# The self stage of an attention and expert kernel rewritten: unnormalised q, x in four parts, early splits of the context weights

## The chip, the cores and the metric

One core of a Trainium2 chip. The metric is device time in microseconds: the time of one execution of the whole program. The core has five engines that run their own instruction streams and meet at semaphores: PE (TensorE, matmuls and transposes), DVE (VectorE), ACT (ScalarE), POOL (GpSimd) and SP (SyncE, which here only issues transfers). PEld is TensorE's loading of weights.

## The reference, cut to what matters

Eight sequences of 256 tokens with 256 features, and for each a context of 1601 rows. The program computes four blocks: grouped-query attention over the tokens and the context, a two-of-eight expert layer, an attention over the context, and a one-of-eight expert layer. The change touches the first block, and a ring of the last. The first block is

```python
x = x + xattn(_layernorm(x), ctx_2048, wq, wk, wv, wo, wk_ctx, wv_ctx, q_norm_w, k_norm_w)

q = rms_norm((x @ wq).reshape(B, L, 16, 128), q_norm_w)     # rsqrt(mean(q*q) + eps) * q * w, for each head
k = rms_norm((x @ wk).reshape(B, L, 4, 128), k_norm_w)
v = (x @ wv).reshape(B, L, 4, 128)
k_ctx, v_ctx = rms_norm(h @ wk_ctx), h @ wv_ctx
q = q * cos + rotate_half(q) * sin
k = k * cos + rotate_half(k) * sin
scores = einsum('blhd,bmhd->bhlm', q, concat(k_ctx, k)) / sqrt(128) + mask
out = einsum('bhlm,bmhd->blhd', softmax(scores), concat(v_ctx, v)) @ wo
```

The rotation is linear in q, and the rms of q is one number for a token and a head. It can be applied to q, or to the scores of that token and head.

## The kernel before, in words

The 2048 tokens are 16 tiles of 128. The stages of the first block follow each other, each in a scope of its own; at a scope's end all engines meet, the stores are waited for, and semaphores are cleared.

**Self stage** (`self_projections`, from line 113). It makes q, k and v of the tokens. A matmul in fp32 quality is done as three with operands split into a high and a low part: ACT makes the high part by a copy (`high`, `split_w`), VectorE the low one by a subtraction (`low`, line 332). A tile has five granules (`GRAN`): j = 0 is k (and v beside it), j = 1 to 4 are four heads of q each, 512 columns a granule. For a granule, TensorE makes `ps_p` (`project`), ACT squares it head by head with a sum (line 239), POOL turns the sums into `rms` by a power of -0.5 (lines 372 and 376), VectorE multiplies `ps_p` by `rms` into `normed` (line 294), makes two halves `by_sin` (line 302) and one head of `by_cos` (line 308), POOL the other three heads of `by_cos` (line 383), VectorE adds them into `roped` (line 317), TensorE transposes it into `ps_t` (line 450), ACT copies that to `out_t` (line 249), and SP stores it in HBM. Each engine's order is written out by hand, with TensorE four granules ahead (`LEAD`), seven of eight tile pairs inside or beside a hardware loop. Before the first granule x (one transfer) gets its statistics, and SP has issued all weights and tables in a row.

**Constants.** A short block of its own casts three constant matrices for later stages (lines 2553 to 2561).

**Context stage** (`context_projections`, from line 472). It loads and splits its weights `w_raw`, `w_hi`, `w_lo`, and does for 104 tiles of context rows: project k and v (twelve matmuls), square (line 589), sum (650), root on POOL (703 and 707), normalise (657), four transposes (745), copy with the weight of k as a scale (597), copy of v (592), stores. Its last two bodies of four tiles split `wo` beside that.

**Attention** (`attention`, from line 806), written out for 32 pairs of sequence and k head. It begins by splitting the first q, k and v. A unit is two heads of one tile of 128 tokens, 128 units in all, eight slots each. For a head, TensorE makes scores in four pieces (lines 1138 to 1143), VectorE takes the maximum of each piece (983) and of the four with a minus sign (`neg_max`, 990), ACT makes four exponentials with `neg_max` as bias (899), POOL divides by the sum (1083), TensorE transposes (1156), ACT and VectorE split (911, 1009), and TensorE multiplies with v (1176 to 1178). The score piece p of a head waits for the exponential p of the head before it. In slots 3 and 7 of a unit the fourth piece of a head is made; in slot 7 it stands right behind the third on TensorE. In slot 6 of even units VectorE also adds the projected output to x (`add_y`, 1025).

**Last stage** (`moe_slots`, from line 2353): 23 slots of 128 rows. POOL gathers the rows of a slot into `xg` and scatters `made`; a gather of slot s + 4 is issued behind the scatter of slot s (`RING = LEAD = 4`), and VectorE's normalise of slot s + 2 (2485), which waits for the gather, stands ahead of the copy `ht` (2511) that TensorE's output product `ps_y` (2435) needs.

Of the kernel before, what the change touches and what calls it, by code (L numbers as in the profile page):

```python
# [10 lines left out]
ALU = mybir.AluOpType  # L11
# [98 lines left out]
LN_EPS, RMS_EPS = 1e-5, 1e-6  # L110


def self_projections(nc, x_sb, x_loaded, ident_loaded, half_made, w_dram, rope_dram, qw_dram, kw_dram, q_dram, k_dram, v_dram,
                     mean_var, rstd, half, ident):
    wq_d, wk_d, wv_d = w_dram
    with ExitStack() as ctx:
        sb, psum, sem = scope(ctx, nc)
        norm = norm_memory(sb, sem, "norm1")
        w_raw = sb("w1_raw", [P, DC, W1])
        w_hi = sb("w1_hi", [P, DC, W1], F32R)  # L120
        w_lo = sb("w1_lo", [P, DC, W1], F32R)
        rope = sb("rope", [P, 2, QT, HD])
# [6 lines left out]
        sq_sum = sb("sq_sum1", [P, GRAN, GRP])  # L129
        sq_mean = sb("sq_mean1", [P, GRAN, GRP])  # L130
        rms = sb("rms1", [P, GRAN, GRP])
        normed = sb("normed1", [P, GRAN, GRP * HD])
        by_cos = sb("by_cos", [P, GRAN, GRP * HD])
        by_sin = sb("by_sin", [P, GRAN, GRP * HD])
        roped = sb("roped", [P, GRAN, GRP * HD])
# [7 lines left out]
        tab_loaded = sem("tab_loaded")  # L143
        w_hi_done, w_lo_done = sem("w1_hi_done"), sem("w1_lo_done")
# [4 lines left out]
        square_done, mean_done, rms_done = sem("square1"), sem("mean1"), sem("rms1s")  # L149
        normed_done, cos_done, sin_done, roped_done = sem("normed1s"), sem("cos1"), sem("sin1"), sem("roped1")  # L150
        t_done, copied, sum_taken = sem("t1_done"), sem("t1_copied"), sem("sum1_taken")
        v_copied, store_begun = sem("v1_copied"), sem("store1_begun")
# [3 lines left out]
        NB = NT // 2  # L156
        LAST = NB - 1
        WPIECES = W1 // 512
        w_loaded = [sem(f"w1_loaded{j}") for j in range(WPIECES)]

        def granule(f):

            return (f // GRAN) % 2, f % GRAN
# [6 lines left out]
        LEAD = 4  # L170
        LASTG = 2 * GRAN
        CH = 3

        def exists(f, last):
            return not (last and f >= LASTG)

        with nc.Block() as block:
            @block.sync
            def _(sp):
                w_rows = [w.rearrange("(c p) n -> p c n", p=P) for w in (wk_d, wv_d, wq_d)]  # L180
                for j in range(WPIECES):
                    src = w_rows[j] if j < 2 else w_rows[2][:, :, (j - 2) * 512:(j - 1) * 512]
                    sp.dma_start(w_raw[:, :, j * 512:j * 512 + 512], src).then_inc(w_loaded[j], 16)
# [2438 lines left out]
```

## Time and profile before

| | us |
|---|---|
| Median of 3 runs | 3123.14 |
| Lowest and highest | 3123.08, 3124.46 |
| The profiled execution, its own time | 3123.67 |
| Its span in the profile | 3121.9 |
| PE busy | 2891.9 (93%) |
| DVE busy | 2181.1 (70%) |
| ACT busy | 2030.9 (65%) |
| POOL busy | 1612.4 (52%) |

Busy time is summed over an engine's instructions, where they overlap once. Matmuls are pipelined, so a busy PE says that it had work, and not how fast it went. The gap between the span and the execution's own time lies before the first and behind the last recorded instruction.

### The profile page before, as it was taken

How to read it: one execution, taken by the hardware profiler on the slowest of the kernel's cores; microseconds unless marked ns; L12 is line 12 of the kernel's file. 1: busy time of each engine (PE TensorE's matmuls, PEld its weight loads, DVE VectorE, ACT ScalarE, POOL GpSimd, SP SyncE). 2: the span in 40 equal slices, each digit the busy share in tenths (PEclk: the TensorE clock that was granted, in tenths of full speed). 3: DMA queues.
4: the chain of work that ended last, by engine and by line, in shares of the span. 5: the costliest groups of instructions: out<-in, count | busy, mean ns of one | idle time of the engine just before them, and what ended most of it. 6: DMA issues, size and time to landing. Idle time of an engine off the chain costs nothing. (4 is left out here: it accounts for less than half of the span.)

```text
span 3121.9 us, 61580 instructions
## 1 busy us (share of the span) xinstructions
PE 2891.9 (93%) x18731; PEld 2450.3 (78%) x18731; DVE 2181.1 (70%) x4611; ACT 2030.9 (65%) x5169; POOL 1612.4 (52%) x2087
## 2 busy tenths in 40 slices
PE   5887999899999999999999999999999977699698
PEld 4665888678888888888888888888888854388654
DVE  7995444577777777777777777777777767766443
ACT  5664666677777777777777777777777647666111
POOL 6993333455555555555555555555555344465122
PEclk9998999999999999999999999999999979899699
DMA  4335666610110110110110110110110010353511
GB/s 134 116 118 175 202 202 203 201 62 33 52 46 33 53 46 33 52 46 33 53 46 33 52 46 33 53 46 33 53 46 33 1 46 1 99 158 113 177 33 28
DMA packets 244462, 236.02 MB, mean 76 GB/s; under 512 B 11654, under 2 KB 224527, under 8 KB 244208
## 3 DMA queue, kind: packets, MB, share of 16 engines
q1 hardware_dynamic: 225552, 212.01, 20.7%
q10 hardware_dynamic: 16448, 15.73, 1.7%
q0 software_dynamic: 2208, 5.12, 0.6%
q8 instruction: 132, 2.16, 0.3%
q14 instruction: 122, 1.00, 0.1%
HBM read 148.93 MB, written 84.80 MB: 75 GB/s over the span
## 5 line engine op out<-in xcount | busy, mean ns | idle before, releaser
L911 ACT ACTIVATE pt_hi<-ps_t 128x512 fp32r<-128x512 f32 (+2 forms) x1024 | 570.4, 557 | 412.9 <-PE ps_t L1156 409.7
L983 DVE TENSOR_REDUCE piece_max<-ps_s 128x1 f32<-128x512 f32 (+2 forms) x1024 | 631.7, 622 | 257.1 <-PE ps_s L1143 229.5
L1009 DVE TENSOR_TENSOR pt_lo<-ps_t,pt_hi 128x512 fp32r<-128x512 f32 (+2 forms) x1024 | 656.4, 641 | 200.5 <-ACT pt_hi L911 184.3
L1083 POOL TENSOR_SCALAR prob<-prob,inv_sum 128x512 f32<-128x512 f32 (+2 forms) x1024 | 639.4, 645 | 268.5 <-DVE inv_sum L999 268.5
L899 ACT ACTIVATE prob<-ps_s,neg_max 128x512 f32<-128x512 f32 (+2 forms) x1024 | 649.2, 634 | 87.6 <-DVE neg_max L990 70.9
L1176 PE MATMUL ps_o<-pt_hi,v_hi 128*128 128x256 f32 (+1 forms) x1856 | 595.4, 321 | 0.0
L1156 PE MATMUL ps_t<-ident,prob 128*128 128x128 f32 (+1 forms) x3712 | 571.9, 272 | 1.4 <-DVE pt_lo L1009 1.3
L1178 PE MATMUL ps_o<-pt_hi,v_lo 128*128 128x256 f32 (+1 forms) x1856 | 523.2, 282 | 0.0
L1177 PE MATMUL ps_o<-pt_lo,v_hi 128*128 128x256 f32 (+1 forms) x1856 | 522.3, 281 | 0.0
L1156 PEld LDWEIGHTS ps_t<-ident,prob 128*128 128x128 f32 (+1 forms) x3712 | 456.2, 140 | 60.7 <-issue 1.6
L1138 PE MATMUL ps_s<-k_hi,q_hi 128*128 128x512 f32 (+2 forms) x1024 | 403.8, 394 | 35.0 <-ACT prob L899 20.0
L1143 PE MATMUL ps_s<-k_hi,q_lo 128*128 128x512 f32 (+2 forms) x1024 | 397.0, 388 | 0.0
L1139 PE MATMUL ps_s<-k_lo,q_hi 128*128 128x512 f32 (+2 forms) x1024 | 376.9, 368 | 0.0
L1177 PEld LDWEIGHTS ps_o<-pt_lo,v_hi 128*128 128x128 f32 (+1 forms) x1856 | 353.6, 191 | 0.0
L1176 PEld LDWEIGHTS ps_o<-pt_hi,v_hi 128*128 128x128 f32 (+1 forms) x1856 | 352.0, 190 | 0.0
L1178 PEld LDWEIGHTS ps_o<-pt_hi,v_lo 128*128 128x128 f32 (+1 forms) x1856 | 349.9, 189 | 0.0
L1091 POOL TENSOR_TENSOR k_lo<-raw_k,k_hi 128x480 fp32r<-128x480 f32 x124 | 150.0, 1219 | 251.3 <-ACT k_hi L918 251.3
L1098 POOL TENSOR_TENSOR v_lo<-raw_v,v_hi 128x512 fp32r<-128x512 f32 (+1 forms) x128 | 155.1, 1220 | 241.2 <-ACT v_hi L925 241.1
L1138 PEld LDWEIGHTS ps_s<-k_hi,q_hi 128*128 128x128 f32 x1024 | 194.3, 190 | 75.3 <-ACT prob L899 55.7
L1143 PEld LDWEIGHTS ps_s<-k_hi,q_lo 128*128 128x128 f32 x1024 | 197.0, 192 | 22.8
L899 ACT ACTIVATION_READ_ACCUMULATOR prob<-ps_s,neg_max 128x1 f32 x1024 | 208.8, 204 | 0.0
L1139 PEld LDWEIGHTS ps_s<-k_lo,q_hi 128*128 128x128 f32 x1024 | 195.1, 191 | 2.9
(262 smaller groups left out, 5621.4 us busy)
## 6 DMA issues: line engine op xcount, KB each, us to landing
v_scratch<-v_out SPq DMA_DIRECT2D x120, 256.0 KB, 2.5
raw_k<-k_scratch SPq DMA_DIRECT2D x32, 960.0 KB, 5.3
raw_v<-v_scratch SPq DMA_DIRECT2D x32, 960.0 KB, 4.7
k_scratch<-k_out SPq DMA_DIRECT2D x104, 256.0 KB, 2.6
q_scratch<-out_t SPq DMA_DIRECT2D x64, 256.0 KB, 2.6
raw_q<-q_scratch SPq DMA_DIRECT2D x32, 512.0 KB, 3.3
c_raw<-in_ctx_t ACTq DMA_DIRECT2D x52, 256.0 KB, 2.8
raw_t<-in_ctx_t SPq DMA_DIRECT2D x24, 512.0 KB, 4.1
```

The lines of the kernel that those rows point to most:

```text
L899: nc.scalar.activation(prob[:, n % PB, lo:hi], ps_s[:, p, lo - p * PC:hi - p * PC], ACT.Exp, bias=neg_max[:, n % PB:n % PB + 1], accum_out ...
L911: nc.scalar.activation(pt_hi[keys, k % RING, cols], ps_t[keys, k % 2, cols], ACT.Copy).then_inc(hi_done, 1)
L983: nc.vector.tensor_reduce(piece_max[:, n % 2, p:p + 1], ps_s[:, p, lo - p * PC:hi - p * PC], AX.X, ALU.max).then_inc(max_ready, 1)
L1009: nc.vector.tensor_tensor(pt_lo[keys, k % RING, cols], ps_t[keys, k % 2, cols], pt_hi[keys, k % RING, cols].bitcast(F32), ALU.subtract).th ...
L1083: nc.gpsimd.tensor_scalar(prob[:, n % PB, lo:hi], prob[:, n % PB, lo:hi], inv_sum[:, n % PB:n % PB + 1], 1.0, ALU.mult, ALU.mult).then_inc ...
L1138: nc.tensor.matmul(out, q_hi[:, gi, h, qs], k_hi[:, gi, lo:hi], start=True, stop=False)
L1139: nc.tensor.matmul(out, q_hi[:, gi, h, qs], k_lo[:, gi, lo:hi], start=False, stop=False)
L1143: nc.tensor.matmul(out, q_lo[:, gi, h, qs], k_hi[:, gi, lo:hi], start=False, stop=True).then_inc(scores_ready, 1)
L1156: last = nc.tensor.transpose(ps_t[0:keys, k % 2, at:at + P], prob[:, (2 * u + j) % PB, blk * P:blk * P + keys], ident[:, :])
L1176: nc.tensor.matmul(out, v_hi[keys, gi, vs], pt_hi[keys, k % RING, cols], start=blk == (0 if qt else 1), stop=False)
L1177: nc.tensor.matmul(out, v_hi[keys, gi, vs], pt_lo[keys, k % RING, cols], start=False, stop=False)
L1178: last = nc.tensor.matmul(out, v_lo[keys, gi, vs], pt_hi[keys, k % RING, cols], start=False, stop=blk == KB - 1)
```

## The change

- q isn't normalised in the self stage. `rotate` becomes `turn`, which for q reads `ps_p` directly; `roped` is added on POOL; only k has a root there. The sums of squares of q (two heads by ACT, two by a reduction on VectorE) are kept for all tiles. In the context stage POOL makes from them, behind the roots of its first body, `q_rms` and its negative by three operations over all 16 x 16 numbers a partition.
- In attention the exponentials get `q_rms` as scale. The negative maximum is the maximum times the negative `q_rms`: VectorE takes the maximum of the first three pieces and its product (`part_max`, `part_neg`) behind the third piece, and joins the fourth to it in one operation.
- x comes in four parts, ordered ahead of and behind the weights; the tables of the rotation are issued from ACT's queue; the weight splits go to VectorE and POOL; the stage is written out without a loop, with k as the second granule of a tile on VectorE.
- The context weights and the first two pairs of context tiles are loaded and split inside the self stage, in tiles 4 to 10. They lie in memory that attention uses for `pt_hi`, `pt_lo`, `o_hi` and `o_lo` later.
- The constants are cast inside the context stage; the first q, k and v of attention are split in its last three bodies, beside `wo`.
- `RING` of `moe_slots` is 6.

```diff
-                def rotate(i, f):
...
-                    nc.vector.tensor_tensor(normed[:, j, :].rearrange("p (h d) -> p h d", h=GRP),
...
-                def add_parts(i, f):
...
-                    nc.vector.tensor_tensor(roped[:, j, :], by_cos[:, j, :], by_sin[:, j, :], ALU.add).then_inc(roped_done, 1)
...
+                def sum_squares(f):
+                    t, j = f // GRAN, f % GRAN
+                    dve.wait_ge(square_done, 3 * (f + 1))
+                    nc.vector.tensor_reduce(sq_sum[:, t, j, 2:4], squares[:, f % 2, 2 * HD:4 * HD].rearrange("p (h d) -> p h d", h=2),
+                                            AX.X, ALU.add).then_inc(reduced, 1)
+
+                def turn(g):
...
+                    else:
+                        dve.wait_ge(square_done, 3 * (f + 1))
+                        made = ps_p[:, j, :]
...
+                    nc.vector.tensor_tensor(by_cos[:, g % RB, :].rearrange("p (h d) -> p h d", h=GRP), made.rearrange("p (h d) -> p h d", h=GRP),
+                                            table[:, which, 0, tt, :].unsqueeze(1).to_broadcast([P, GRP, HD]), ALU.mult).then_inc(turned, 1)
...
+                def add_parts(g):
+                    pool.wait_ge(turned, 3 * (g + 1))
+                    if g >= RB:
+                        pool.wait_ge(t_done, g - RB + 1)
+                    nc.gpsimd.tensor_tensor(roped[:, g % RB, :], by_cos[:, g % RB, :], by_sin[:, g % RB, :], ALU.add).then_inc(roped_done, 1)
...
+                root_x(0)
+                root_x(1)
+                low_w(2)
+                pool.wait_ge(tab_loaded, 16 * 8)
...
+                load_x(0)
+                sp.dma_start(ident[:, :], ident_dram).then_inc(ident_loaded, 16)
                 for j in range(WPIECES):
...
+                for n in range(1, X_PARTS):
+                    load_x(n)
...
+                for j in range(2):
+                    sp.wait_ge(w_lo_done[j], 1)
+                for n, src in enumerate(ctx_w_dram):
+                    sp.dma_start(w2_raw[:, :, n * 512:n * 512 + 512], src.rearrange("(c p) n -> p c n", p=P)).then_inc(w2_loaded, 16)
...
+                nc.gpsimd.tensor_scalar(q_negative[:, :, :], q_rms[:, :, :], 1.0 / HD, RMS_EPS,
+                                        ALU.mult, ALU.add).then_inc(q_mean_done, 1)
+                pool.wait_ge(q_mean_done, 1)
+                nc.gpsimd.tensor_tensor(q_rms[:, :, :], q_negative[:, :, :], half[:, 0:NH].unsqueeze(1).to_broadcast([P, NT, NH]), ALU.pow).then_inc(q_rms_done, 1)
+                pool.wait_ge(q_rms_done, 1)
+                nc.gpsimd.tensor_scalar(q_negative[:, :, :], q_rms[:, :, :], -1.0, 1.0, ALU.mult, ALU.mult).then_inc(q_scaled, 1)
...
-                                         bias=neg_max[:, n % PB:n % PB + 1],
+                                         bias=neg_max[:, n % PB:n % PB + 1], scale=scale_of(i, n, q_rms),
...
+                def part_maximum(i, n):
+
+                    dve.wait_ge(max_ready, i * 64 + 4 * n + 3)
+                    nc.vector.tensor_reduce(part_max[:, n % 2:n % 2 + 1], piece_max[:, n % 2, 0:3], AX.X, ALU.max).then_inc(part_ready, 1)
+                    dve.wait_ge(part_ready, i * 16 + n + 1)
+                    nc.vector.tensor_scalar(part_neg[:, n % 2:n % 2 + 1], part_max[:, n % 2:n % 2 + 1], scale_of(i, n, q_negative), None,
+                                            ALU.mult).then_inc(part_neg_ready, 1)
+
                 def negative_maximum(i, n):
                     dve.wait_ge(max_ready, i * 64 + 4 * n + 4)
+                    dve.wait_ge(part_neg_ready, i * 16 + n + 1)
...
-                    nc.vector.tensor_reduce(neg_max[:, n % PB:n % PB + 1], piece_max[:, n % 2, :], AX.X, ALU.max,
-                                            negate=True).then_inc(neg_max_ready, 1)
+                    nc.vector.scalar_tensor_tensor(neg_max[:, n % PB:n % PB + 1], piece_max[:, n % 2, 3:4], scale_of(i, n, q_negative),
+                                                   part_neg[:, n % 2:n % 2 + 1], ALU.mult, ALU.min).then_inc(neg_max_ready, 1)
...
+        def operands_at(i, t):
+
+            if not isinstance(i, int) or i < NB - END_BODIES:
+                return []
+            at = (i - NB + END_BODIES) * TB + t
+            first_n = at + (at + 1) // 2
+            return range(first_n, first_n + 2 - at % 2)
...
-    RING = 4
+    RING = 6
```

## Rows read from the trace of the kernel before

**Rows 1.** Windows: stretch, length, busy time of each engine, clock, DMA.

```profile
core 0: us, PE busy (x) PEld busy (x) DVE busy (x) ACT busy (x) POOL busy (x), PEclk, DMA share, GB/s
32.00:253.00 221.00, 181.69 (x886) 132.13 (x885) 216.06 (x425) 141.55 (x721) 196.71 (x235) 0.97 0.36 110
269.00:606.00 337.00, 336.64 (x1656) 275.56 (x1656) 164.77 (x260) 212.09 (x368) 124.33 (x206) 1.00 0.70 210
641.00:2505.00 1864.00, 1843.46 (x13318) 1660.65 (x13318) 1393.54 (x2985) 1371.86 (x3483) 1010.31 (x1326) 1.00 0.11 41
```

**Rows 2.** Groups by form in 0 to 250 us: busy us, mean ns.

```profile
L302 DVE TENSOR_TENSOR by_sin<-normed,rope_w 128x256 f32<-128x256 f32 x158 | 88.4, 599 | 2.7
...
L294 DVE TENSOR_TENSOR normed<-ps_p,rms 128x512 f32<-128x512 f32 x80 | 54.3, 678 | 1.0 <-POOL rms L376 1.0
```

**Rows 3.** Timeline of the opening: start, duration, engine, instruction.

```profile
9.12 1.87 SPq L185 DMA_DIRECT2D rope<-in_rope  x2
...
29.63 0.76 DVE L302 TENSOR_TENSOR by_sin<-normed,rope_w 128x256 f32<-128x256 f32 x2
30.31 0.28 DVE L308 TENSOR_TENSOR by_cos<-normed,rope_w 128x128 f32<-128x128 f32 x1
...
36.92 1.11 PE L450 MATMUL ps_t<-ident,roped 128*128 128x128 f32 x4 [3.91 <-DVE roped L317]
...
41.60 0.60 PE L450 MATMUL ps_t<-ident,roped 128*128 128x128 f32 x4
```

**Rows 4.** Timeline from the self stage to the context stage.

```profile
255.91 0.60 ACT L249 ACTIVATE out_t<-ps_t 128x512 f32<-128x512 f32 x1 [1.27 <-PE ps_t L450]
260.58 0.17 DVE L2556 MEMSET ones_bf<- 128x128 bf16 x1 [7.16 <-PEq L57]
...
269.00 0.77 PE L720 MATMUL ps_k<-w_hi,c_hi 128*128 128x512 f32 x1 [13.13 <-DVE c_lo L643]
```

**Rows 5.** Timelines of ACT and of PE, from the context stage to attention.

```profile
614.74 1.15 ACT L918 ACTIVATE q_hi<-raw_q 128x512 fp32r<-128x512 f32 x2 [3.26 <-PEq L57]
...
622.29 0.66 PE L1138 MATMUL ps_s<-k_hi,q_hi 128*128 128x384 f32 x1 [12.06 <-DVE k_lo L1034]
```

**Rows 6.** Timeline of attention where one unit ends.

```profile
1531.86 0.69 DVE L983 TENSOR_REDUCE piece_max<-ps_s 128x1 f32<-128x512 f32 x1 [0.57 <-PE ps_s L1143]
...
1532.47 0.41 DVE L1025 TENSOR_TENSOR x_sb<-ps_o,x_sb 128x256 f32<-128x256 f32 x1
...
1533.31 0.16 DVE L990 TENSOR_REDUCE neg_max<-piece_max 128x1 f32<-128x4 f32 x1
1533.39 0.15 DVE L995 TENSOR_REDUCE row_sum<-piece_sum 128x1 f32<-128x4 f32 x1
1533.51 0.69 ACT L899 ACTIVATE prob<-ps_s,neg_max 128x512 f32<-128x512 f32 x1 [0.17 <-PE ps_t L1156]
1533.57 0.16 DVE L999 RECIPROCAL inv_sum<-row_sum 128x1 f32<-128x1 f32 x1
...
1534.34 0.50 PE L1138 MATMUL ps_s<-k_hi,q_hi 128*128 128x512 f32 x1 [0.48 <-ACT prob L899]
```

**Rows 7.** The page's costliest groups: a two-input operation on POOL.

```profile
L1098 POOL TENSOR_TENSOR v_lo<-raw_v,v_hi 128x512 fp32r<-128x512 f32 (+1 forms) x128 | 155.1, 1220 | 241.2 <-ACT v_hi L925 241.1
```

**Rows 8.** Groups by form in 300 to 580 us.

```profile
L707 POOL TENSOR_TENSOR rms<-sq_mean,half 128x4 f32<-128x4 f32 x88 | 88.7, 1008 | 12.7 <-POOL sq_mean L703 10.9
...
L597 ACT ACTIVATE k_out<-ps_t,kw_col 128x512 f32<-128x512 f32 x87 | 59.5, 684 | 0.0
...
L592 ACT ACTIVATE v_out<-ps_v 128x512 f32<-128x512 f32 x87 | 52.0, 597 | 68.0 <-PE ps_v L722 68.0
```

**Rows 9.** Last stage: output products on PE (timeline), then a row of the waits.

```profile
2972.39 1.89 PE L2435 MATMUL ps_y<-down_w,ht 128*128 x8
...
2989.85 1.89 PE L2435 MATMUL ps_y<-down_w,ht 128*128 x8
...
3102.27 1.99 PE L2435 MATMUL ps_y<-down_w,ht 128*128 x8 [0.25 <-DVE ht L2511]
...
DVE xn L2485 <- DMA xg<-x_rows_scratch,read_at: 72.4, 20, 4.6
```

More of the change, by code:

```diff
@@ L168, in w_cols, with rotated, turn_of @@
             return slice(at, at + GRP * HD)
[L170 to L175, printed above, removed]
+        def rotated(g):
+            t, j = g // GRAN, ORDER[g % GRAN]
+            return t, j, t * GRAN + j
+        def turn_of(f):
+            return f // GRAN * GRAN + ORDER.index(f % GRAN)
         with nc.Block() as block:
@@ L268, in _ @@
-                body(0, False)
-                with act.Fori(1, LAST) as i:
-                    body(i, False)
-                body(LAST, True)
+                    square(f)
+                for n in range(NG):
+                    if n + LEAD < NG:
+                        square(n + LEAD)
+                    if n % GRAN == 1 and n // GRAN + 2 < NT:
+                        high(n // GRAN + 2)
+                    copy_out(n)
+                    if n % GRAN == 3 and n // GRAN in range(4, 4 + C_PIECES + 2):
+                        high_context(n // GRAN - 4)
@@ L287, in rotate @@
[L287 to L299 removed]
+                nc.vector.memset(half[:, :], -0.5).then_inc(half_made, 1)
@@ new lines, in _ @@
+                normalise(0)
+                low_w(0)
+                low(0)
+                low_w(1)
+                normalise(1)
+                low_w(3)
+                low_w(4)
+                measure(2)
+                measure(3)
+                low(1)
+                dve.wait_ge(table_ready, 5)
+                sum_squares(0)
+                for n in range(NG):
+                    t = n // GRAN
+                    if n % GRAN == 0 and t + 2 < NT:
+                        normalise(t + 2)
+                    if n % GRAN == 2 and t + 4 < NT:
+                        measure(t + 4)
+                    if n % GRAN == 4 and t + 2 < NT:
+                        low(t + 2)
+                    turn(n)
+                    if n + 1 < NG:
+                        sum_squares(n + 1)
@@ L467, in _ @@
-                body(0, False)
-                with pe.Fori(1, LAST) as i:
-                    body(i, False)
-                body(LAST, True)
-def context_projections(nc, ctx_dram, wk_dram, wv_dram, kw_dram, wo_dram, q_dram, k_dram, v_dram, half, ident, operands):
+                transpose_x(0)
+                project(0)
+                transpose_x(1)
+                for f in range(1, LEAD):
+                    project(f)
+                for n in range(NG):
+                    if n % GRAN == 1 and n // GRAN + 2 < NT:
+                        transpose_x(n // GRAN + 2)
+                    if n + LEAD < NG:
+                        project(n + LEAD)
+                    transposes(n)
@@ L626, in body @@
                         copy_k(i, t)
-                        if not loads:
-                            high_wo(t + (TB if last else 0))
+                        for n in operands_at(i, t):
+                            high_operand(n)
                 body(0, False, True)
-                with act.Fori(1, LAST - 1) as i:
+                with act.Fori(1, LAST - 2) as i:
                     body(i, False, True)
+                body(LAST - 2, False, True)
                 body(LAST - 1, False, False)
```

664 lines of the change are left out of this document (324 added, 340 removed).

## The prediction

> **What bounds the kernel now.** I read first the busy time and granted clock by stage [rows 1]. From 641 to 2505 us (the attention) TensorE is busy 1843 of 1864 us at full clock: that stage costs what TensorE's order of work costs. From 269 to 606 us (the context stage) it is busy 336.6 of 337.0 us, 3.24 us for each of 104 tiles. From 32 to 253 us (the self stage) the limit is VectorE, 216.1 of 221 us, while TensorE has 181.7. So a cheaper VectorE pays in the self stage alone; in attention anything between two matmuls pays or costs at once. Then I read groups by form [rows 2], the opening of the self stage [rows 3], the two stage changes [rows 4, 5], one unit boundary of attention [rows 6], the small and pointer operands [rows 7, 8] and the last stage [rows 9].
>
> **Self stage: removed and moved.** Per granule VectorE loses `normed` for q, the part cosine and the add (0.68 to 0.70 us each), and gains a full cosine and a 256-element reduction. Start to start, a 512-column operation takes 0.61 us [rows 6], from 1531.86 to 1532.47 and one of 256 takes 0.34 [rows 3], the pair from 29.63 to 30.31. A q granule is then 0.34 + 0.34 + 0.61 + 0.34 = 1.63 us, the k granule 2.3, and a tile adds 1.3 (normalise, low part, statistics): 4 x 1.63 + 2.3 + 1.3 = 10.1 us. Bound from above: `by_sin` has a mean of 0.599 for operations that take 0.34 alone, while `normed`, which reads PSUM, has 0.678 with GpSimd just as busy [rows 2]; if all ten `by_sin` stayed at 0.599 the tile would be 12.7 us. I take the slow value for k only (+1.0): 11.1. The Trainium skill (SBUF — State Buffer, on the shared port pair) says that VectorE contends with GpSimd when it has two SBUF inputs, and q's operands now lie in PSUM and SBUF; by that rule q would run at 0.34, and the two rows agree with it.
>
> TensorE sets a second floor. A self tile has 36 matmuls of 512 columns and 22 transposes, three context tiles 36 and 12: 3 x 3.24 = 9.7 us, and ten transposes more at up to 0.15 (four last 0.60 [rows 3]): 11.2. GpSimd takes over the add, 1.22 us at 512 columns [rows 7], five times, with one root of k (1.0 + 0.2 + waits, 1.5 [rows 8]) and one of x: about 9 us a tile, 10.3 with a context piece. With three engines this close I take 11.7 us a tile, between 11.2 and 12.9.
>
> Opening: SP issues a quarter of x first, so the first transposition and the weight splits come earlier. Eight table loads move to ACT's queue, ahead of its first split; two of them took 1.87 us to issue on SP [rows 3], so ACT is free at about 8 us. Behind that GpSimd runs in order: a weight piece (2.4, twice 1.22), five table operations (3.8), another piece (2.4), two roots of x and one of k (3.7), the first add (1.2), from about 12 us on: first roped tile at 25.5, first output transposition at 26 instead of 36.92 [rows 3]. From there 79 granules, 15.8 x 11.7 = 185 us, end at 211 instead of 255.9 [rows 4]. **Self stage: -45 us** (-33 to -53). The stores stay on SP, one per granule; its waits for two low weight pieces end near 14 us, before the first store is due.
>
> **Stage change at 256 us.** TensorE waits 13.1 us; the constants' block starts at 260.58 and the first context matmul at 269.00 [rows 4]. With weights and the first two pairs already split, and with the casts moved into a stage where VectorE has 172 of 337 us free, only the stores' landing and the block change remain, to 260.9. **-8 us** (-7 to -10).
>
> **Stage change at 610 us.** ACT begins attention at 614.74, TensorE at 622.29 after splits of q, k and v [rows 5]. These move into the last three bodies of the context stage: 18 pieces over 12 tiles, ACT +0.9 us a tile on 2.0 (212 of 337 us busy), VectorE +0.9 on 1.6, both under 3.24. TensorE could begin at 614.9: -7.4, less 1.4 for delays where ACT gets near its limit. **-6 us** (-3 to -10).
>
> **Last stage.** The ring of gathered rows goes from 4 to 6. Before 2990 the output products follow each other at (2989.85 - 2972.39)/3 = 5.82 us, later at (3102.27 - 2989.85)/17 = 6.61, while VectorE waits 72.4 us in all for `xg` [rows 9]. A gather is issued behind the store of a slot, so two more slots give it 11.6 us. The period goes back to 5.82: 17 x 0.79 = **-13.4 us** (-11 to -14).
>
> **Attention: added.** Per head VectorE gets two operations, `part_max` and `part_neg`, between the third and fourth piece maximum. The next score on TensorE waits for the fourth maximum, the negative maximum and the first exponential, and this chain has no slack where a unit ends: fourth maximum, `neg_max` 1533.31, exponential 1533.51, score 1534.34 after 0.48 us of idle TensorE [rows 6]. Added ahead of the fourth maximum: waiting for the third one's result instead of issuing behind it (its 0.69 must end, where 0.61 sufficed, and a semaphore be seen: 0.12), the second operation behind the first (0.18, as row_sum to reciprocal), the issue of the next (0.09) = 0.39. Each exponential gets a second pointer operand: the copy with one lasts 0.684, without 0.597 [rows 8], +0.09. At the three other kinds of boundary ACT or TensorE takes up 0.00 to 0.12 of that, so 0.44 on average, x 127 units = **+56 us**. If VectorE hides the waits and a second pointer is free: 0.2 x 127 = 25; with 0.1 more for the new form of the last operation and some loss inside the unit: 75. Inside a unit (the fourth slot) VectorE idles before the fourth maximum, and I count nothing.
>
> **The wide power.** All q roots are taken by one GpSimd operation of 256 elements a partition, behind the roots of the first context body. The trace has only the 4-element form: 1.008 us [rows 8]. From below: all of it fixed, 1.0. From above: per element, (1.008 - 0.2)/4 = 0.20, times 256 = 52 us. A plain two-input operation of 512 elements takes only 1.22 us [rows 7], so a fixed part of 0.8 us over it is hard to place, and I take the per-element reading, the one nearest to the row that exists. Queued behind it are the roots of all later tiles; VectorE's `normed` waits for them, and TensorE's in-order transposes wait for that. It can run ahead only about 1.9 us: **+50 us**.
>
> The Trainium skill (GPSIMD Engine Reference, Performance versus the Vector engine) gives about 2.6 cycles an element for a two-input operation and names no exception for a power. As an estimate from that page, 256 elements would be 0.6 us and the kernel would end near 3108 us. The 4-element row at 1.008 us does not look like that rule, and no row here has another width.
>
> **Sum.** Against the profiled execution (span 3121.9, its own time 3123.7, 0.5 above the median of the runs): 3123.7 - 45 - 8 - 6 - 13.4 + 56 + 50 = 3157.3, so 3157 us. Its own range is 3138 to 3175.
>
> **Rivals.**
> - *The power is cheap* (1 to 5 us), a vector loop with a fixed start. For it: the plain operation's slope. Against: 1.008 us for four elements. 3157 - 48 = 3109. This decides the sign: below about 10 us for the power the kernel is faster.
> - *The power costs about 15 us*: 3157 - 36 = 3121, no change.
> - *Attention's chain absorbs the new operations* (a cost of 25 and not 56). Against: the idle TensorE at the boundary. 3126 with the dear power, 3078 with the cheap one.
> - *The self stage couples worse than its engines' sums* (four rope buffers, one transposition bank, ACT's squares waiting for VectorE's sums): 13 us a tile gives back 21 us: 3178.
>
> **How the numbers follow.** Forecast 0.45; cheap power 0.27; 15 us power 0.12; attention absorbed 0.08; self stage not faster 0.08. What this kernel's measurement can tell from no change is about 0.2%, 6 us, so 3117 to 3129. Faster: the cheap power and part of the absorbed case, 0.33; same 0.15; slower 0.52. The range goes from the cheap power with some luck in the self stage to the upper part of the forecast: 3098 to 3172.
>
> **What would show it.** In the new profile: a GpSimd operation with 128x256 elements near 230 us and its length, with a hole in TensorE behind it if it is long; self tiles at 11.7 us; first context matmul about 5 us after the last transposition; attention's 1864 us longer by 56; output products at 5.82 us to the end. The forecast is wrong above all if that one operation is short.

## The result and the profile after

The changed kernel takes 3235.3 us (median of 4 runs, 3232.8 to 3236.4) against 3123.8 for the kernel before on the same chip: ratio 1.0354, 95% interval 1.0339 to 1.0369. It is 112 us slower. The forecast was 3157 us, with a range of 3098 to 3172: slower was right, but by 33 us and not by 112. In the profiled executions the span goes from 3121.9 to 3234.1, also 112.2 us, so the two traces hold the whole difference.

First the stages in the trace after: windows with the stretch, its length, busy time of each engine, clock, DMA (the counterpart of [rows 1]).

```profile
32.00:213.00 181.00, 171.71 (x881) 135.37 (x882) 165.19 (x379) 121.62 (x494) 135.90 (x139) 0.98 0.45 136
219.00:605.00 386.00, 339.13 (x1664) 278.42 (x1664) 175.12 (x281) 218.72 (x380) 170.84 (x211) 0.93 0.63 187
641.00:2605.00 1964.00, 1845.56 (x13056) 1636.87 (x13055) 1511.47 (x3438) 1441.54 (x3430) 992.54 (x1306) 1.00 0.11 39
```

The window of the self stage is 40 us shorter and TensorE is now its busiest engine (171.7 of 181 us). The context stage has TensorE busy for about as long as before, 339 us, in a stretch of 386 instead of 337. In attention TensorE has 118 us of idle time in 1964, where it had 21 in 1864. Now the marks between the stages, from the timelines (start, duration, engine, instruction, idle time before it), against [rows 3 to 5]:

```profile
30.96 0.66 PE L510 MATMUL ps_t<-ident,roped 128*128 128x128 f32 x4 [2.77 <-POOL roped L432]
...
213.50 0.60 ACT L281 ACTIVATE out_t<-ps_t 128x512 f32<-128x512 f32 x1 [1.27 <-PE ps_t L510]
...
218.54 0.77 PE L798 MATMUL ps_k<-w_hi,c_hi 128*128 128x512 f32 x1 [5.07 <-PEq L57]
...
241.71 0.39 PE L800 MATMUL ps_v<-w_hi,c_lo 128*128 128x512 f32 x1
279.16 1.12 PE L823 MATMUL ps_t<-ident,normed 128*128 128x128 f32 x4 [37.06 <-DVE normed L716]
...
605.03 0.66 PE L1223 MATMUL ps_s<-k_hi,q_hi 128*128 128x384 f32 x1 [4.96 <-PEq L57]
```

| From, to | before, us | after, us | difference | forecast |
|---|---|---|---|---|
| start to last copy of the self stage | 255.9 | 213.5 | -42.4 | -45 |
| to the first context product | 13.1 | 5.0 | -8.1 | -8 |
| to the first score of attention | 353.3 | 386.5 | +33.2 | +50 - 6 |
| first score to last output product | 1882.4 | 2026.4 | **+144.0** | **+56** |
| to the first gate product of the last stage | 456.6 | 454.9 | -1.7 | 0 |
| to the end of the span | 160.6 | 147.8 | -12.8 | -13.4 |

The differences add to 112.2. All rows but one are within 11 us of the forecast; attention is off by 88. The hole of 37.06 us in TensorE is the wide power. These are groups by form over the whole span: count, then busy time and mean ns of one. (The trace names the buffer `sq_sum`, in whose memory `q_rms` lies.)

```profile
L785 POOL TENSOR_TENSOR sq_sum<-q_negative,half 128x256 f32<-128x256 f32 x1 | 41.6, 41562 | 0.1
L412 POOL TENSOR_TENSOR rstd<-var_eps,half 128x1 f32<-128x1 f32 x16 | 8.9, 556 | 1.3
```

One element takes 0.556 us, four take 1.01 [rows 8], 256 take 41.56: (41.56 - 1.01)/252 = 0.161 us an element over a fixed 0.4.

Attention shows its loss at the places that the prediction named, and at some that it did not. This is one unit end in the timeline of all engines after, beside [rows 6]:

```profile
1618.55 0.69 DVE L1063 TENSOR_REDUCE piece_max<-ps_s 128x1 f32<-128x512 f32 x1
1618.94 2.25 POOL L1187 TENSOR_TENSOR v_lo<-raw_v,v_hi 128x512 fp32r<-128x512 f32 x2 [2.66 <-ACT v_hi L1009]
...
1619.27 0.16 DVE L1069 TENSOR_REDUCE part_max<-piece_max 128x1 f32<-128x3 f32 x1
1619.46 0.21 DVE L1071 TENSOR_SCALAR part_neg<-part_max,q_negative 128x1 f32<-128x1 f32 x1
1619.59 0.41 DVE L1114 TENSOR_TENSOR x_sb<-ps_o,x_sb 128x256 f32<-128x256 f32 x1
1619.92 0.48 DVE L1063 TENSOR_REDUCE piece_max<-ps_s 128x1 f32<-128x321 f32 x1
...
1620.44 0.77 DVE L1079 SCALAR_TENSOR_TENSOR neg_max<-piece_max,q_negative,part_neg 128x1 f32<-128x1 f32 x1
...
1621.25 0.67 ACT L983 ACTIVATE prob<-ps_s,neg_max,sq_sum 128x384 f32<-128x384 f32 x1 [1.07 <-DVE neg_max L1079]
...
1622.06 0.45 PE L1223 MATMUL ps_s<-k_hi,q_hi 128*128 128x384 f32 x1 [1.01 <-ACT prob L983]
```

Two things are to be seen. `part_max` and `part_neg` push the add back: it starts 1.04 us behind the third maximum, where it was 0.61 in [rows 6], so 0.43 us later (forecast 0.39), and the fourth maximum with it. And the join `neg_max`, an operation on one element a partition, takes 0.77 us here. It ends at 1621.21; GpSimd's subtraction beside it ends at 1618.94 + 2.25 = 1621.19. At the next head, inside a unit, it is 1.21 us, and again ends with GpSimd's subtraction. One such place, from the timelines of GpSimd and of VectorE, where the subtraction of k ends at 1566.57 and the join at 1566.59:

```profile
1564.18 2.39 POOL L1180 TENSOR_TENSOR k_lo<-raw_k,k_hi 128x480 fp32r<-128x480 f32 x2 [2.97 <-ACT k_hi L1002]
```

```profile
1565.38 1.21 DVE L1079 SCALAR_TENSOR_TENSOR neg_max<-piece_max,q_negative,part_neg 128x1 f32<-128x1 f32 x1
```

Elsewhere the same operation takes 0.22. The line's own view (count, then minimum, median and maximum ns) covers all of them:

```profile
L1079 DVE SCALAR_TENSOR_TENSOR neg_max<-piece_max,q_negative,part_neg x256: 218/219/1214, 610.7 to 2609.9; 128x1 f32<-128x1 f32 x128
```

The timelines from 1000 to 2000 us have 128 joins, and 80 of them start beside a subtraction of GpSimd. Where that has 0.01 to 0.12 us to go the join still takes 0.22; where it has 0.73 to 0.76 to go, 0.76 to 0.77; where it has 1.19 to 1.20 to go, 1.20 to 1.21. `part_neg`, which starts beside the same subtraction above, takes its usual 0.21. No join of these starts beside GpSimd's one-input `normalise`, so what that would do is not shown.

### The profile page after: what moved, and what is told of

The parts are those of the page before. It is cut to its first block and busy times, and to the rows that moved or that the text cites. A ratio compares the mean times of both kernels' runs of the same rounds, so it can differ in the third digit from the quotient of the medians.

```text
span 3234.1 us, 60539 instructions
## 1 busy us (share of the span) xinstructions
PE 2917.4 (90%) x18731; PEld 2467.0 (76%) x18731; DVE 2267.5 (70%) x5052; ACT 2100.0 (65%) x4929; POOL 1592.2 (49%) x1993
## 5 line engine op out<-in xcount | busy, mean ns | idle before, releaser
L983 ACT ACTIVATE prob<-ps_s,neg_max,sq_sum 128x512 f32<-128x512 f32 (+2 forms) x1024 | 740.7, 723 | 199.7 <-DVE neg_max L1079 193.6
L1098 DVE TENSOR_TENSOR w_lo<-ps_t,w_hi 128x512 fp32r<-128x512 f32 (+2 forms) x1024 | 655.9, 641 | 218.1 <-ACT w_hi L995 206.2
L995 ACT ACTIVATE w_hi<-ps_t 128x512 fp32r<-128x512 f32 (+2 forms) x1024 | 569.0, 556 | 351.8 <-PE ps_t L1241 344.4
L1261 PE MATMUL ps_o<-w_hi,v_hi 128*128 128x256 f32 (+1 forms) x1856 | 595.3, 321 | 0.0
L1263 PE MATMUL ps_o<-w_hi,v_lo 128*128 128x256 f32 (+1 forms) x1856 | 523.2, 282 | 0.0
L1262 PE MATMUL ps_o<-w_lo,v_hi 128*128 128x256 f32 (+1 forms) x1856 | 522.5, 282 | 0.0
L1261 PEld LDWEIGHTS ps_o<-w_hi,v_hi 128*128 128x128 f32 (+1 forms) x1856 | 351.9, 190 | 3.9
L1262 PEld LDWEIGHTS ps_o<-w_lo,v_hi 128*128 128x128 f32 (+1 forms) x1856 | 353.5, 190 | 0.0
L1263 PEld LDWEIGHTS ps_o<-w_hi,v_lo 128*128 128x128 f32 (+1 forms) x1856 | 350.1, 189 | 0.0
L983 ACT ACTIVATION_READ_ACCUMULATOR prob<-ps_s,neg_max,sq_sum 128x1 f32 x1024 | 205.0, 200 | 0.0
```

Source lines behind the costliest of these rows:

```text
L983: nc.scalar.activation(prob[:, n % PB, lo:hi], ps_s[:, p, lo - p * PC:hi - p * PC], ACT.Exp, bias=neg_max[:, n % PB:n % PB + 1], scale=sca ...
L995: nc.scalar.activation(pt_hi[keys, k % RING, cols], ps_t[keys, k % 2, cols], ACT.Copy).then_inc(hi_done, 1)
L1098: nc.vector.tensor_tensor(pt_lo[keys, k % RING, cols], ps_t[keys, k % 2, cols], pt_hi[keys, k % RING, cols].bitcast(F32), ALU.subtract).th ...
L1261: nc.tensor.matmul(out, v_hi[gi][keys, vs], pt_hi[keys, k % RING, cols], start=blk == (0 if qt else 1), stop=False)
L1262: nc.tensor.matmul(out, v_hi[gi][keys, vs], pt_lo[keys, k % RING, cols], start=False, stop=False)
L1263: last = nc.tensor.matmul(out, v_lo[gi][keys, vs], pt_hi[keys, k % RING, cols], start=False, stop=blk == KB - 1)
```

## The experiments

Each run is timed beside the kernel before on its chip, and compared by its median with the 3235.3 us of the change; medians of the kernel before were 3125 to 3126 in these jobs, so differences of 1 to 2 us between jobs mean nothing. The diffs are shortened: operands stand without their indices, and waits and semaphores are mostly left out.

**1. `ptr_join`: the same join without a second tensor.**

```diff
-nc.vector.scalar_tensor_tensor(neg_max, piece_max[3], scale_of(i, n, q_negative), part_neg, ALU.mult, ALU.min)
+nc.vector.tensor_scalar(neg_max, piece_max[3], scale_of(i, n, q_negative), part_neg, ALU.mult, ALU.min)
```

> The changed kernel with the join of the negative maximum as one operation on one tensor and two pointer operands (piece maximum times q_negative, minimum with part_neg) in place of scalar_tensor_tensor with two tensors in SBUF; same arithmetic. Theory A (a VectorE operation with two SBUF tensors is held until the running GpSimd operation ends): the join lasts about 0.22 us at every boundary, the 0.77 and 1.21 us ones are gone, and at two of eight boundaries per four units 0.55 and 0.99 us come back: 32 x 1.54 = 49 us, so 3235 - 49 = 3186 us. Theory B (the join is long there because of what it waits for, or because of its position in VectorE's queue): the same two joins stay at 0.77 and 1.21 us and the time at 3235.

3202.9 us, ratio to before 1.0248 (1.023 to 1.0265). The join, by its line's view in 700 to 2500 us:

```profile
L1079 DVE TENSOR_SCALAR neg_max<-piece_max,q_negative,part_neg x233: 271/273/277, 700.4 to 2492.9; 128x1 f32<-128x1 f32 x117
```

No join is longer than 0.28 us, though GpSimd subtracts beside it as before. Theory B is out. The gain is 32 us and not 49, in part because the second pointer operand costs 0.05 us at each of the 256 joins. That it is the second tensor, and not the form scalar_tensor_tensor, is settled by experiment 7.

**2. `attn_as_before` and `scale_only`: attention without its new operations, and with the scale operand alone.** Both take the maximum in one operation again; `attn_as_before` also drops the scale, so q's rms is applied nowhere.

```diff
-                        if p == 2:
-                            part_maximum(0, n)
...
-                                if sp == 2:
-                                    part_maximum(i, n)
...
-nc.vector.scalar_tensor_tensor(neg_max, piece_max[3], scale_of(i, n, q_negative), part_neg, ALU.mult, ALU.min)
+nc.vector.tensor_reduce(neg_max, piece_max, AX.X, ALU.max, negate=True)
```

> The changed kernel with attention's arithmetic on the maximum and the exponential as in the kernel before: no part_max, part_neg or join, one reduction over the four piece maxima, no scale operand; q stays unnormalised, so the rows of q are not divided by their root mean square. All of the growth of the attention stage (2026.4 - 1882.4 = 144 us from its first score to its last output product) comes from these operations: the stage goes back to 1882 and the time to 3235 - 144 = 3091 us. Rival: some of it comes from where the operands now lie or from the new first units; then it stays above 3100.

> As the run with attention as before, but the exponentials keep q_rms as their scale; the maximum is not multiplied by it, so the exponents are shifted wrongly. It prices the second pointer operand alone. Prediction on record: 0.09 us at each unit end, 128 x 0.09 = 12 us over attention as before, 3103 us. Rival: ScalarE is short of time inside the units as well, and all eight exponentials of a unit count where their banks are awaited: up to 1024 x 0.089 = 91 us if every one counted, about 37 us if it explains what the predicted 0.44 per unit and the long joins leave open (142 - 56 - 49), so 3128 us.

`attn_as_before`: 3090.0 us (0.9886, 0.9869 to 0.9902). That is 145 us less, so the 144 us are all in the new operations; memory places and first units cost nothing. `scale_only`: 3113.2 us (0.9962, 0.9948 to 0.9976). So the second pointer operand costs 23.2 us by the medians (19.9 by the spans of the two profiled executions), about twice the forecast, and the part operations with the join 3235.3 - 3113.2 = 122.

My expectation calls the exponents of `scale_only` shifted wrongly. That was a mistake: the shift is the same for a whole row and cancels in the division by the row's sum, so this is still the softmax, without one product. What it needs is that (`q_rms` - 1) times the raw maximum stays in the range of an exponential. With the inputs of this kernel it does; with others that has to be bounded first.

**3. `split_power`: the power in 32 pieces of 8 elements.**

```diff
-nc.gpsimd.tensor_tensor(q_rms[:, :, :], q_negative[:, :, :], half..., ALU.pow)
...
+                for i in range(1, NB):
+                    for t in range(TB):
+                        root(i, t)
+                        if done < len(pieces):
+                            n, h = pieces[done]
+                            cols = slice(h * H8, (h + 1) * H8)
+                            nc.gpsimd.tensor_tensor(q_rms[:, n, cols], q_negative[:, n, cols], half[:, 0:H8], ALU.pow)
+                            done += 1
```

> The changed kernel with the one power over 256 elements cut into 32 powers of 8 elements, one behind the root of each of the next 32 context tiles. One piece should last (41.56 / 256) x 8 + 0.2 = 1.5 us, GpSimd then has 0.2 + 1.0 + 1.5 and its waits in 3.24 us a tile. Theory A: TensorE's hole of 37.1 us goes whole, 3235 - 37 = 3198 us. Theory B: the roots behind each piece come late and every one of 32 tiles stretches by some 0.5 us: 3214 us.

GpSimd's loop over the bodies is written out for it. 3196.3 us (1.0228, 1.0211 to 1.0245), 39.0 less. Groups by form on GpSimd in 200 to 420 us, then TensorE's transposes in the context stage:

```profile
L794 POOL TENSOR_TENSOR sq_sum<-q_negative,half 128x8 f32<-128x8 f32 x32 | 52.4, 1636 | 0.0
```

```profile
L831 PE MATMUL ps_t<-ident,normed 128*128 128x128 f32 x416 | 63.0, 274 | 5.6 <-DVE normed L716 5.6
```

The pieces take 52.4 us together, more than the whole, and cost no time that these runs show, since GpSimd has it between its roots; TensorE waits 5.6 us for `normed` in the stage where it waited 41.9. The context stage alone, from its first product to attention's first score, took 386.5 us in the changed kernel and takes 347.0 here (216.4 to 563.4): the hole cost 2.4 us more than its 37.06. Windows of the changed kernel (as above), and rows of TensorE's timeline ahead of the hole and behind it, show a reason:

```profile
242.00:279.00 37.00, 0.10 (x1) 0.00 (x0) 0.59 (x1) 0.60 (x1) 35.73 (x4) 0.57 0.03 9
279.00:286.00 7.00, 6.84 (x23) 5.59 (x24) 4.34 (x11) 1.99 (x4) 2.79 (x4) 0.57 0.43 112
```

```profile
240.12 0.40 PE L799 MATMUL ps_k<-w_lo,c_hi 128*128 128x512 f32 x1
240.35 0.39 PE L800 MATMUL ps_k<-w_hi,c_lo 128*128 128x512 f32 x1
...
280.93 0.63 PE L800 MATMUL ps_k<-w_hi,c_lo 128*128 128x512 f32 x1
281.35 0.63 PE L798 MATMUL ps_k<-w_hi,c_hi 128*128 128x512 f32 x1
```

The granted clock is 0.57 in the hole, near the lower of its two levels (1.2 of 2.4 GHz), and still 0.57 over the 7 us behind it, when TensorE is at work again. Its products start 0.42 us apart there, and 0.23 ahead of the hole. From one group of four transposes to the next the tile behind the hole takes 285.09 - 279.16 = 5.93 us, the one ahead of it 238.75 - 235.56 = 3.19: that is 2.7 us. In `split_power` the clock is 1.00 from 242 to 279 us.

**4. `ring4`: the ring of the last stage back to 4.**

```diff
-    RING = 6
+    RING = 4
```

> The changed kernel with RING = 4 in the last stage. The prediction's term for the ring was 13.4 us, and from the first gate product to the last product of the last stage the traces show 151.5 us before and 138.5 after. If that is the ring's doing: 3235 + 13 = 3248 us, and VectorE again waits some 70 us for xg. If the stage was helped by something else (where its buffers lie, what runs ahead of it), 3235.

3248.3 us (1.0396, 1.0378 to 1.0413), 13.1 more. The waits of VectorE in the last stage (us in all, times, longest), with 4 and then with 6:

```profile
DVE xn L2570 <- DMA xg<-x_rows_scratch,read_at: 76.3, 21, 5.1
```

```profile
DVE xn L2570 <- DMA xg<-x_rows_scratch,read_at: 6.1, 2, 5.2
```

**5. `split_no_product`: 2 and 3 together.** Its edit is that of `scale_only` and of `split_power`.

> The two repairs together: q_rms as scale with the reduction over four piece maxima as before (no product with q_negative; the shift of the exponents cancels in the division by the row sum), and the power in 32 pieces. If they add up: 3113.2 - 39.0 = 3074 us, 1.6% under the kernel before. If GpSimd or TensorE's lead was hiding one in the other: above 3080.

3075.0 us (0.9842, 0.9826 to 0.9859). They add up: 3074 was expected.

**6. `split_late_product`: the product once, at the end of the chain.**

```diff
+nc.vector.tensor_reduce(part_max, piece_max, AX.X, ALU.max).then_inc(part_ready, 1)
+dve.wait_ge(part_ready, i * 16 + n + 1)
+nc.vector.tensor_scalar(neg_max, part_max, scale_of(i, n, q_negative), None, ALU.mult).then_inc(neg_max_ready, 1)
```

> Power in 32 pieces, and the product with q_negative once, behind the reduction over all four maxima (two operations at the end of the chain, none ahead of the fourth maximum). Theory: each unit end is later by one small product and its wait, 0.21 us, or 128 x 0.21 = 27 us over the version without a product: 3101 us. Rival: inner boundaries count too (256 x 0.21 = 54 us): 3128 us. The form of the change costs 90 us there with no join held by GpSimd (3202.9 - 3113.2), so both would be under it.

3130.0 us (1.0018, 1.0008 to 1.0028): 55 over the version without a product, which is 0.21 us for each of 256 heads. The rival (3128) was right. A head that ends inside a unit costs as much as one that ends it: 0.20 to 0.26 us each in the table below, but for the last unit end with 0.06.

**7. `late_product_two_tensors`: the same product on two tensors.**

```diff
-nc.vector.tensor_scalar(neg_max, part_max, scale_of(i, n, q_negative), None, ALU.mult)
+nc.vector.tensor_tensor(neg_max, part_max, scale_of(i, n, q_negative), ALU.mult)
```

> As the version with 32 pieces and the late product (3130.0 us), with the product as tensor_tensor: part_max and a column of q_negative as two tensors in SBUF, in place of one tensor and a pointer. Same place in the order, same result. Theory A (a VectorE operation with two SBUF tensors is held to the end of the GpSimd operation that runs): in the trace of the late product GpSimd is in a subtraction at three of eight products of a cycle of four units, with 0.35, 1.00 and 1.17 us to go, so these three last up to that long; less 0.05 us each for a pointer that isn't read: about +1.5 us a cycle, 32 cycles, +48 us: 3178 us. Theory B (only scalar_tensor_tensor does this): 0.16 us each, 256 x 0.05 less: 3117 us.

3180.4 us (1.0175, 1.0158 to 1.0192); the expectation said 3178. The longest of them, from the timelines of GpSimd and of VectorE:

```profile
1449.70 2.40 POOL L1185 TENSOR_TENSOR k_lo<-raw_k,k_hi 128x480 fp32r<-128x480 f32 x2 [2.97 <-ACT k_hi L1010]
```

```profile
1450.93 1.18 DVE L1088 TENSOR_TENSOR neg_max<-part_max,q_negative 128x1 f32<-128x1 f32 x1
...
1458.49 0.16 DVE L1088 TENSOR_TENSOR neg_max<-part_max,q_negative 128x1 f32<-128x1 f32 x1
```

So theory A of experiment 1 holds, and it isn't the form scalar_tensor_tensor. A product of one element lasts 0.16 us, or until GpSimd's subtraction ends (1452.10; the product 1452.11). From 1000 to 2000 us 48 of 128 products are longer, each ending within 0.03 us of its subtraction: three of every eight, as expected.

**8. `split_early_max`: the maximum of three ahead of the fourth, no product there.**

```diff
-nc.vector.tensor_scalar(part_neg, part_max, scale_of(i, n, q_negative), None, ALU.mult)
...
+nc.vector.tensor_scalar(neg_max, piece_max[3], part_max, scale_of(i, n, q_negative), ALU.max, ALU.mult)
```

> Power in 32 pieces; the maximum of three pieces ahead of the fourth as in the change, but no product there, and the join as one operation with two pointers (maximum with part_max, times q_negative). Against the late product it moves one small operation (0.16 us and its wait on the third maximum, 0.3 in all) ahead of the fourth maximum, and the join is 0.27 instead of 0.16 and 0.21. If everything VectorE issues there counts, wherever it stands: 0.3 + 0.11 per head over the version without a product, 256 x 0.41 = 105 us, less what hides inside units: between 3140 and 3180 us. If the early position hides the reduction, as its authors would want: 256 x 0.11 = 28 us over 3075, 3103 us.

3119.9 us (0.9979, 0.9969 to 0.9988), 45 over the version without a product and between the two expectations: the early place hides some of it, and leaves 0.18 us a head. Inside units it leaves 0.07 to 0.12 (table below), about the 0.11 by which the join with two pointers is longer than the reduction: the early maximum costs nothing there. At three of the four unit ends it leaves 0.26 to 0.30. It is the fastest version measured that keeps the exact product.

**9. `late_add` and `early_add`: VectorE's add of the output product into x, in slot 7 and in slot 5 instead of 6.**

```diff
-                            if s == 6 and u % 2 == 0 and u > 0:
+                            if s == 5 and u % 2 == 0 and u > 0:
...
-                            elif s == 6 and u == 0 and positive(i):
+                            elif s == 5 and u == 0 and positive(i):
```

> As the version without a product and with 32 pieces, with VectorE's add of the output product into x moved from slot 6 to slot 7 of every other unit, behind the negative maximum. The add takes 0.41 us ahead of the fourth maximum at two of four unit ends. If it stands on the chain there, up to 64 x 0.4 = 26 us: 3050 us. If the fourth maximum waits for its score anyway at those ends: 3074 us.

> As the version without a product and with 32 pieces (3075.0 us), with VectorE's add of the output product into x in slot 5 of every other unit instead of slot 6. One slot later it cost 46.6 us, with TensorE waiting for it before the next products. If the add stands on the chain to the fourth maximum at these unit ends and slot 5 has 0.41 us free: up to 64 x 0.2 = 13 us less, 3062 us. If it waits there for its product, or the fourth maximum waits for its score: 3075 us or more.

`late_add`: 3121.7 us (0.9986, 0.9976 to 0.9996), 46.6 slower. In the code, TensorE's products of every other unit wait for the add (`y_added`). The view of its waits has 57.7 us ahead of these products, in 58 waits, under a releaser that the profile can't name ("issue"); `split_no_product` has no such row. In the timeline one of them starts 0.11 us behind the end of VectorE's add (1420.03 to 1420.44):

```profile
PE ps_o L1264 <- issue: 57.7, 58, 1.3
```

```profile
1420.55 0.36 PE L1264 MATMUL ps_o<-w_hi,v_hi 128*128 128x256 f32 x1 [0.99 <-issue]
```

`early_add`: 3063.0 us (0.9798, 0.9782 to 0.9815), 12.0 less than `split_no_product`, as expected, and the fastest version here: 2.0% under the kernel before. Its cycle of eight heads takes 58.70 us and not 59.10, or 13 us in 32 cycles.

**10. `add_on_vector`: the add of the rotated parts back on VectorE.**

```diff
-nc.gpsimd.tensor_tensor(roped, by_cos, by_sin, ALU.add)      # add_parts
+nc.vector.tensor_tensor(roped, by_cos, by_sin, ALU.add)      # in turn, behind by_cos
```

> The changed kernel with the add of the rotated parts back on VectorE, in the self stage; GpSimd keeps the roots. VectorE is busy 165.2 of 181 us there, 10.5 us a tile of 11.6; five adds of 512 elements at 0.61 to 0.69 us are 3.1 to 3.5 us more, so 13.6 to 14 us a tile, and the stage is longer by 15.8 x (13.8 - 11.6) = 35 us: 3270 us. Rival: VectorE's by_cos and normalise of x lose their waits for GpSimd's adds (normalise 1.11 us where 0.41 is its own) and half comes back: 3250 us.

3266.2 us (1.0448, 1.0431 to 1.0466), 31 slower. Its window of the self stage, and k's sine product there and in the changed kernel (groups by form):

```profile
32.00:240.00 208.00, 171.74 (x871) 132.80 (x870) 204.44 (x450) 120.49 (x492) 34.86 (x60) 0.98 0.39 115
```

```profile
L373 DVE TENSOR_TENSOR by_sin<-normed,rope_w 128x256 f32<-128x256 f32 x30 | 11.4, 422 | 0.5
```

```profile
L373 DVE TENSOR_TENSOR by_sin<-normed,rope_w 128x256 f32<-128x256 f32 x30 | 16.1, 575 | 0.5
```

VectorE is the bound again (204 of 208 us). And `by_sin` of k, whose two operands lie in SBUF, falls from 0.575 to 0.422 us once GpSimd adds nothing beside it.

## Where the 144 us of attention come from

TensorE's order in attention repeats after four units, eight heads. The table (columns by run; `no_product`, `late_product`, `two_tensors` and `early_max` are the runs of 5 to 8) gives for each head the time from the start of its fourth score piece to that of the next head's, read from TensorE's timeline between 1400 and 1540 us; odd rows cross a boundary inside a unit, even rows the end of one. There are 32 such cycles.

```
head        before  change  ptr_join  no_product  late_product  two_tensors  early_max
1 inside      6.52    6.59      6.64        6.55          6.78         6.73       6.65
2 unit end    7.37    8.48      7.99        7.43          7.69         8.49       7.73
3 inside      6.32    7.50      6.56        6.32          6.52         7.48       6.39
4 unit end    8.69    9.25      9.30        8.78          8.99         8.94       9.04
5 inside      6.47    6.63      6.69        6.56          6.82         6.75       6.68
6 unit end    7.66    8.25      8.31        7.75          7.99         7.94       8.05
7 inside      6.69    7.02      7.07        6.82          7.07         6.99       6.93
8 unit end    8.78    9.21      9.22        8.89          8.95         9.10       9.00
cycle        58.50   62.93     61.78       59.10         60.81        62.42      60.47
```

- **The scale operand:** 59.10 - 58.50 = 0.60 a cycle, 19 us (23.2 by the medians). `attn_as_before` has 58.48, so the cycle of the kernel before is back there.
- **The part operations and a join that nothing holds:** 61.78 - 59.10 = 2.68 a cycle, 86 us (89.7 by the medians). At the four unit ends it is 0.56 + 0.52 + 0.56 + 0.33 = 1.97, at the four inner boundaries 0.09 + 0.24 + 0.13 + 0.25 = 0.71. The join's own 0.11 (0.27 against 0.16 for the reduction) is in each of them.
- **The held join:** 62.93 - 61.78 = 1.15 a cycle, 37 us (32.4 by the medians). It is in heads 2 and 3 alone, 0.49 and 0.94; elsewhere the join with two pointers is the slower one, by 0.28 in all. So the wait itself is 1.43 a cycle, 46 us, of which `ptr_join` spends 9 on its second pointer.

Together 4.43 x 32 = 142 us, of 144.0 in the trace.

## Why the prediction was wrong, by its own steps

- **Self stage, -45:** measured -42.4, mechanism as told. The first output transposition came at 30.96 and not at 26, since GpSimd's first weight piece waited for ACT's split and began at 16.25, not at the 12 us that I had (timeline of the changed kernel):

```profile
16.25 2.35 POOL L417 TENSOR_TENSOR w_lo<-w_raw,w_hi 128x1024 fp32r<-128x1024 f32 x1 [8.59 <-ACT w_hi L250]
18.56 4.78 POOL L452 TENSOR_TENSOR rope_w<-rope,norm_w 128x256 f32<-128x256 f32 x4
...
29.65 1.26 POOL L432 TENSOR_TENSOR roped<-by_cos,by_sin 128x512 f32<-128x512 f32 x1
```

  From there to the last transposition at 212.38 a tile took 181.4/15.8 = 11.5 us, forecast 11.7. The claim that VectorE's load set the stage, and that the add had to leave it, is borne out by `add_on_vector`. The sine products of q stayed fast: 0.410 us mean against 0.575 for k's. The working on them was loose all the same: it set a mean duration (0.599) against a spacing (0.34), while the shortest of them lasts 0.409 us in the trace before, so the surplus of k's two is 0.4 us a tile and not the 1.0 that I added. VectorE was busy 165.2/15.8 = 10.5 us a tile and not 11.1; the 11.7, set by hand above TensorE's floor, was right without that term.
- **Stage changes, -8 and -6:** -8.1 for the first. The second lies in one stretch with the power's hole; `split_power`, which has no hole, takes 347.0 us there against 353.3 before: -6.3.
- **Last stage, -13.4:** -12.8 in the trace, 13.1 by `ring4`. The output products start 5.82 us apart, as forecast ((3214.41 - 3115.47)/17 in the timeline).
- **The wide power, +50:** 39.0. The reading per element was right: 0.161 us each, where I had 0.20. TensorE also ran on to 242.1 us, 7.5 us behind the start of the power at 234.55, and not 1.9.
- **Attention, the part operations:** "this chain has no slack where a unit ends" was right, and the 0.39 us nearly so: the add behind them is late by 0.43. Three parts of the step failed. The join was taken to last as long as the reduction that it replaces (the 0.1 for it stands only in the upper bound); free of GpSimd it is 0.06 longer, and 0.11 with two pointers. The discount for "the three other kinds of boundary", which no row bears out, was too large: in `ptr_join` three of the four kinds of unit end lose 0.61 to 0.65 us against the kernel before, pointer included, and the fourth 0.44, where the sum had 0.44 on average. And "Inside a unit (the fourth slot) VectorE idles before the fourth maximum, and I count nothing" is wrong: inner boundaries cost 0.71 us a cycle, 23 us in all, and in `split_late_product` as much as unit ends. Idle time ahead of the fourth maximum hides nothing that stands behind it, and not all that stands ahead: one early operation is hidden inside units (`split_early_max`), while two leave 0.13 us over the join's own 0.11 at two of the four inner boundaries (`ptr_join`). By which wait an inner delay reaches TensorE was not isolated.
- **Attention, the pointer, 0.09 at unit ends:** the price was right (an exponential takes 723 ns on average against 634), its number was not: 19 to 23 us and not 11. Inner boundaries count here too. The Trainium skill (ScalarE: Activation LUTs, What ACT_TABLE_LOAD costs) puts a pointer operand at about 93 ns, and the trace agrees with 89.
- **The held join:** not in the prediction at all, 32 to 37 us. I named the shared port for the self stage and did not ask the question of the three small operations in attention. One of them, the join, has two tensors in SBUF. A subtraction of GpSimd (of q, k or v) is running when it starts at five boundaries of every eight, and has more than the join's own time to go at two of them. `ptr_join` takes the second tensor away and the wait goes; `late_product_two_tensors` puts one in and it comes back. The Trainium skill (SBUF — State Buffer, Who interferes with whom) says that a VectorE instruction with two SBUF inputs contends with a GpSimd instruction that reads SBUF, and that the contention for the shared ports is an exclusive lock. The runs agree for GpSimd's two-input subtractions: 1.21 us for one element, ending 0.02 us behind the subtraction. `part_neg`, with one tensor and a pointer, is at most 0.22 us everywhere in 700 to 2572 us.

So the sum failed in one term: +56 for attention measured +144, as 23 for the pointer (11 forecast), 90 for the part operations and join (45 forecast) and 32 for a lock that was not forecast. The power, 11 us cheaper than forecast, made the miss smaller; that was luck. The cheap-power rival, to which 0.27 had gone, is out. Without the wide power and the new operations on the maximum, the gains of 42.4 + 8.1 + 6.3 + 13.1 = 70 us were there to be had. `early_add` is 62.7 us under the kernel before of its own job: it pays about 20 for the pointer and gets 12 from the place of the add.

## What to carry to other kernels

Count a small operation behind the last wait of a critical chain at its full price on every trip, and look for its second tensor in SBUF before its length: beside a two-input GpSimd operation it can last as long as that one still has to go. Before moving a factor into the bias of a softmax, ask whether the bias needs it: a shift common to the row cancels, and here the product, with the wait that its join brought, cost more than the whole rewrite gained. A long operation on an in-order queue can be cut into pieces that fit its gaps: here that took away the whole cost, though the pieces take more time together (52.4 against 41.6 us).

## What the runs showed of the hardware

- A power on GpSimd costs 0.161 us an element over a fixed 0.4 (1, 4, 8 and 256 elements: 0.556, 1.01, 1.64, 41.56 us), while a plain two-input operation of 512 elements takes 1.22 [rows 7]. The Trainium skill's 2.6 cycles an element (GPSIMD Engine Reference, Performance versus the Vector engine) does not hold for it; the measurement decides.
- A VectorE operation of one element with two SBUF tensors, 0.16 or 0.22 us alone, lasted up to 1.21 us, to the end of GpSimd's two-input subtraction; with one tensor and pointers it never lasted over 0.28.
- On VectorE each pointer operand of a one-element operation costs 0.05 us: 0.16, 0.21 and 0.27 us with none, one and two.
